# Second score and aggregation of later chunks behind the adjacency products; a leaving state added to x one half step later

## The chip, the cores and the metric

The kernel runs on one core of one Trainium2 chip. The metric is device time in microseconds, the median over runs of the whole program. TensorE does matrix products and transposes into PSUM, VectorE and ScalarE move and combine what stands there, POOL (GpSimd) does small work in SBUF, SyncE issues transfers.

## What is computed

Four layers on x of shape (128, 64, 256), each on a normalised, rectified copy of x and added to x: two attention layers with 8 heads, then a graph attention, then three steps of a gated recurrence. The change touches the last two. Cut from the reference:

```
h = maximum(layernorm(x), 0)                     # third layer
h = h @ W
s1, s2 = h @ a1, h @ a2
e = leaky_relu(s1[:, :, None] + s2[:, None, :], 0.2) * mask
x = x + elu(softmax(e) @ h + beta * h)
h = maximum(layernorm(x), 0)                     # fourth layer
for _ in range(3):
    av = concat([adj @ h, adj @ h])
    z = sigmoid(lin(av, w3) + lin(h, u3))
    r = sigmoid(lin(av, w4) + lin(h, u3))
    hv = tanh(lin(av, w5) + lin(r * h, u5))
    h = (1 - z) * h + z * hv
x = x + h
```

## The kernel before

The 8192 rows are 64 tiles of 128, taken as 16 chunks of 4 tiles. The first two layers run over all chunks (to about 610 us). The graph layer of chunks 0 and 1 is done on the way, and that of chunks 2 to 15 inside the recurrence. Every fp32 product is made as three products of high and low parts (`product`, L91), so one 256x256 weight on a chunk is 12 matmuls of 512 columns. ScalarE writes the high part, VectorE the low part (`..._hi`, `..._lo`).

The recurrence works on 8 groups of two chunks, in halves. A group has 6 halves (k = 1 to 5, then 0 of the next group; `Half`, L395), two for each of the three steps; even k belongs to the first chunk of the group, odd k to the second. While TensorE makes the sums of one chunk, the gates of the other are finished: each `half` ends half k-1's state with u5 and begins its own half with u3. The order on each engine is written out by hand in one function `half` per engine (ScalarE L898, VectorE L1360, TensorE L1759); `Half` says which chunk's graph work goes into which half. Engines wait for each other by counting semaphores alone.

On TensorE a half is: transposes of the state (halves 2 to 5, `ring` banks 0 and 1), u3 (12 matmuls, `ring` banks 2 and 3, named hu afterwards), adjacency (64 matmuls of 64x64 tiles into `scores`, L1706), u5 on r*h of the other chunk, w4 (sum of r, `ring` 0 and 1), w3 (sum of z, `scores` 0 and 1), w5 (`scores` 2 and 3). Between these stand the graph pieces of a later chunk: `graph_rows` (transposes, L1659), `graph_product` for four tiles (the product with W and both score columns, `g_hT` with `g_w`, alternately in `ring` 2 and 3), `graph_s2` (the second score spread over rows, 16 matmuls of 64x64 tiles, L1671), `graph_attT` (4 transposes of the attention, L1679), `graph_aggregate` (16 matmuls of 64x64 tiles, attT with hw, L1690). A chunk that enters the recurrence is transposed by `enter` (L1648), one that leaves by L1847.

On VectorE: `r*h` (L1369) and rh_lo, `graph_low`, `agg_low`, statistics for a normalisation (`rows_stats`, L1203), `update` of the state in two parts (L1322 to L1327, three operations each), `r_sum`, the low part of h (L1397), `z_sum`, `graph_scores` (L1226 to L1235: sum, leaky relu, mask, maximum), `graph_attention` (L1239 to L1246: total, reciprocal, att), `copy_attT` (L1253), `graph_positive` and `graph_negative` (y added to x), `leave` (state added to x). On ScalarE: copies of the transposed state (`tok`, printed as later_w), rhp_hi, tanh of z, copies hu, `graph_high`, `agg_high`, tanh of hv, `copy_hw` (L827), high part of h, `r_tanh` (L881), `graph_read` and `graph_exp` (y), `norm_rows`. POOL shifts the scores by their maximum (`g_shift`) and makes the scale of a normalisation.

## Time and profile before

| what | value |
|---|---|
| median of 3 runs | 1502.7 us (1502.57 to 1502.71) |
| the profiled execution's own time | 1503.36 us |
| its span | 1501.6 us |
| TensorE matmul busy, share of the span | 98% |
| TensorE weight load | 82% |
| VectorE | 83% |
| ScalarE | 66% |
| POOL | 36% |
| mean granted TensorE clock | 0.991 of full speed |

Busy times are sums over the span; a matmul's end is modelled and matmuls overlap, so pitches are read from the starts in the timeline. A wait of TensorE shows as idle time in front of a row, with what ended it behind an arrow. In the rows `ring` and `scores` are the two PSUM tensors; `later_w` is the memory that tok, z and the exponential of y share.

### The profile page before, as it was taken

To read this page: it belongs to the slowest core of one execution; us is meant where nothing else is said; L and a number is where in the kernel's file an instruction comes from. 1 tells how busy PE (TensorE), PEld (TensorE's weight loads), DVE (VectorE), ACT (ScalarE), POOL (GpSimd) and SP (SyncE) were. 2 spreads that over 40 slices of the span, in tenths; PEclk is the share of its full clock that TensorE was granted. 3 is DMA by queue.
4 is the path that set the end of the run, shared out by engine and by line. 5 is a ranking of instruction groups with operands and counts; after the bars stand their busy time and mean duration, and the time that the engine had idled before them with its cause. 6 is when DMAs were issued, how large, how long until landed. Compare 5 with 4: busy or idle time off the path is not lost.

```text
span 1501.6 us, 45862 instructions
## 1 busy us (share of the span) xinstructions
PE 1464.4 (98%) x18922; PEld 1237.2 (82%) x18922; DVE 1244.5 (83%) x2517; ACT 990.1 (66%) x1795; POOL 538.7 (36%) x623
## 2 busy tenths in 40 slices
PE   8999999899999997799999999999999999999997
PEld 7898999899888886688888788887887887887886
DVE  4888877989999998888888888888888888888767
ACT  5767767667777776666666666666666666666564
POOL 3876776767888885411101101111111111111000
PEclk9999999999999999899999999999999999999999
DMA  8300000002333234100000000000000000000000
GB/s 267 87 2 0 0 0 2 16 17 45 65 68 65 56 58 59 29 1 1 29 1 2 30 1 1 30 1 1 30 1 1 30 1 1 29 2 1 29 2 28
DMA packets 36839, 40.89 MB, mean 27 GB/s; under 512 B 11872, under 2 KB 31840, under 8 KB 36704
## 3 DMA queue, kind: packets, MB, share of 16 engines
q0 software_dynamic: 4608, 16.78, 5.9%
q1 hardware_dynamic: 32096, 22.10, 4.9%
q8 instruction: 111, 1.82, 0.5%
q14 instruction: 24, 0.20, 0.0%
HBM read 13.71 MB, written 8.39 MB: 15 GB/s over the span
## 4 chain that ended last, share of the span: by engine, by line
PE 91%; DVE 5%; ACT 1%; POOL 1%; issue 1%; DMA 0%; DVEq 0%; POOLq 0%
PE ring L99 43%; PE scores L99 28%; PE scores L1706 3%; PE ring L1506 3%; PE scores L1470 3%; PE ring L1546 2%; PE ring L1775 2%; PE ring L1517 2%; PE ring L1690 1%; PE ring L1847 1%; PE ring L1648 1%; PE ring L1659 1%; PE ring L1671 1%; DVE s L1035 1%; PE ring L1679 0%
## 5 line engine op out<-in xcount | busy, mean ns | idle before, releaser
L543 POOL TENSOR_TENSOR s<-s,mx 128x512 f32<-128x512 f32 x128 | 138.2, 1103 | 56.8 <-DVE mx L1040 56.8
L617 POOL TENSOR_TENSOR r_var_eps<-r_mean_var,eps 128x4 f32<-128x4 f32 x16 | 8.1, 508 | 377.1 <-DVE r_mean_var L1208 377.1
L549 POOL TENSOR_TENSOR s<-s,rtotal 128x512 f32<-128x512 f32 x128 | 130.8, 1059 | 31.6 <-DVE rtotal L1046 31.4
L701 ACT ACTIVATE s<-s 128x512 f32<-128x512 f32 x128 | 77.9, 642 | 69.0 <-POOL s L543 68.8
L1371 DVE TENSOR_TENSOR rhp_lo<-r,rhp_hi 128x1024 fp32r<-128x1024 f32 x47 | 57.6, 1225 | 73.4 <-ACT rhp_hi L916 73.4
L1035 DVE SCALAR_TENSOR_TENSOR s<-scores,mask 128x512 f32<-128x512 f32 x128 | 87.1, 681 | 30.6 <-PE scores L1470 30.6
L881 ACT ACTIVATE r<-r,bias_half 128x512 f32<-128x512 f32 x96 | 64.3, 717 | 58.9 <-DVE r L1342 58.9
L935 ACT ACTIVATE hv<-scores,bias 128x512 f32<-128x512 f32 x94 | 64.7, 689 | 55.0 <-PE scores L99 55.0
L909 ACT ACTIVATE later_w<-ring 128x512 f32<-128x512 f32 x64 | 34.8, 596 | 99.0 <-PE ring L1775 99.0
L713 ACT ACTIVATE pT<-ring 128x512 f32<-128x512 f32 x128 | 66.1, 603 | 42.4 <-PE ring L1506 42.4
L1040 DVE TENSOR_REDUCE mx<-s 128x8 f32<-128x512 f32 x128 | 87.9, 686 | 4.4
L1333 DVE TENSOR_TENSOR agg_lo<-scores,agg_hi 128x512 fp32r<-128x512 f32 x96 | 61.8, 685 | 32.7 <-ACT agg_hi L874 32.3
L1044 DVE TENSOR_REDUCE total<-s 128x8 f32<-128x512 f32 x128 | 82.5, 645 | 0.0
L99 PE MATMUL ring<-agg_hi,w4T_hi 128*128 128x512 f32 x192 | 78.2, 407 | 2.3 <-DVE agg_lo L1333 2.3
L99 PE MATMUL scores<-rhp_hi,u5T_hi 128*128 128x512 f32 (+1 forms) x192 | 80.3, 418 | 0.0
L99 PE MATMUL scores<-agg_hi,w5T_hi 128*128 128x512 f32 (+1 forms) x192 | 78.3, 408 | 0.0
L617 POOL TENSOR_TENSOR g_var_eps<-g_mean_var,eps 128x4 f32<-128x4 f32 x16 | 8.3, 519 | 192.7 <-DVE g_mean_var L1208 192.7
L99 PE MATMUL scores<-agg_hi,w3T_hi 128*128 128x512 f32 x192 | 77.2, 402 | 0.0
L99 PE MATMUL scores<-agg_hi,w3T_lo 128*128 128x512 f32 x192 | 75.8, 395 | 0.0
L99 PE MATMUL scores<-agg_lo,w3T_hi 128*128 128x512 f32 x192 | 75.8, 395 | 0.0
L99 PE MATMUL ring<-agg_hi,w4T_lo 128*128 128x512 f32 x192 | 75.8, 395 | 0.0
L99 PE MATMUL ring<-agg_lo,w4T_hi 128*128 128x512 f32 x192 | 75.7, 394 | 0.0
(314 smaller groups left out, 5129.8 us busy)
## 6 DMA issues: line engine op xcount, KB each, us to landing
x<-beta_less_one POOLq DMA_DIRECT2D x16, 512.0 KB, 4.7
x<-o POOLq DMA_DIRECT2D x16, 512.0 KB, 6.6
out_x<-x SPq DMA_DIRECT2D x15, 512.0 KB, 2.9
x<-in_x SPq DMA_DIRECT2D x1, 6144.0 KB, 25.4
later_w<-in_L_gnn_w_w SPq DMA_DIRECT2D x3, 512.0 KB, 6.4
x<-in_x SPq DMA_DIRECT2D x2, 512.0 KB, 5.3
x<-in_x SPq DMA_DIRECT2D x1, 1024.0 KB, 7.4
stage<-in_L_gnn_w_qkv SPq DMA_DIRECT2D x3, 256.0 KB, 3.1
```

The source lines that it names most:

```text
L99: last = pe.matmul(out, s, m, start=(begins and n == 0), stop=(ends and n == len(terms) - 1))
L543: pool.tensor_tensor(sr, sr, mx[:, r, :].unsqueeze(2).to_broadcast([P, CT * 2, N]), ALU.subtract).then_inc(s_shifted, 1)
L549: pool.tensor_tensor(sr, sr, rtotal[:, r, :].unsqueeze(2).to_broadcast([P, CT * 2, N]), ALU.mult).then_inc(p_ready, 1)
L701: act.activation(s[:, par, r, :, :, :], s[:, par, r, :, :, :], ACT.Exp).then_inc(p_exp, 1)
L713: act.activation(pT[:, r, :, :].rearrange("p t q -> p (t q)"), ring[:, r, :], ACT.Copy).then_inc(pT_copied, 1)
L881: act.activation(r[:, m, :], r[:, m, :], ACT.Tanh, bias=bias_half[:, 1, m:m + 1], scale=0.5)\
L935: act.activation(hv[:, m, :], high[:, 2 + m, :], ACT.Tanh, bias=bias[:, 2, m:m + 1])\
L1035: dve.scalar_tensor_tensor(sr(par, r), scores[:, r, :].rearrange("p (a k) -> p a k", k=N), SCALE, masks[layer_of(i, lay)][:].unsqueeze(1). ...
L1040: dve.reduce_max(mx[:, r, :], sr(par, r), AX.X).then_inc(s_max, 1)
L1044: dve.reduce_sum(total[:, r, :], sr(par, r), AX.X).then_inc(p_total, 1)
L1333: dve.tensor_tensor(agg.lo[:].rearrange("p m (t g q) -> p g m t q", t=CT, g=2)[:, g], high[:, g, :].rearrange("p (m t q) -> p m t q", m=FT ...
L1371: dve.tensor_tensor(rhp.lo[:], r[:], f32(rhp.hi[:]), ALU.subtract).then_inc(rh_lo_ready, 1)
```

## The change

In `Half`, the second score and the attention of a chunk (`graph_s`) stay in halves 2 and 4, the aggregation and all behind it (`graph_b`) move to halves 3 and 5. `graph_s2` and `graph_aggregate` stand right behind the adjacency products. The transposes of the attention stand behind w5 in `ring` bank 3, where u3 of the next half writes its second part. In halves with graph products w4 comes first, then two graph products, w3, two graph products, w5; ScalarE makes all four copies of hw behind tanh of r. ScalarE copies hu in front of each tanh of z. The final transposes of a leaving state stand behind w5 in banks 0 and 1, and VectorE adds them to x in the next half, between r*h and rh_lo. Statistics of a chunk for the recurrence come behind the low part of h (half 3) or the sum of z (half 5); the odd chunk's rows are normalised in half 0 and not in half 5.

The diff, cut to the table of halves and to the functions `half` of ScalarE, VectorE and TensorE. Left out are the first half of all (a semaphore of its own for its copies of hu), waits that moved from helpers to their callers, and `final_rows`, which holds the loop of the final transposes as before with the bank as an argument.

```diff
-self.left = group * 2 - 2 if self.k == 0 and not self.first else None
-self.left_before = group * 2 - 1 if self.k == 1 and not (fixed and group == 0) else None
+self.left = None
+if self.k == 0 and not self.first:
+    self.left = group * 2 - 2
+if self.k == 1 and not (fixed and group == 0):
+    self.left = group * 2 - 1
 self.later = group * (HALVES - 2) + self.k
 self.before_step = STEPS - 1 if self.k == 0 else (self.k - 1) // 2
...
 even, odd = group * 2 + 2, group * 2 + 3
 self.graph_a = {1: even, 3: odd}.get(self.k) if goes_on else None
-self.graph_b = {2: even, 4: odd}.get(self.k) if goes_on else None
+self.graph_s = {2: even, 4: odd}.get(self.k) if goes_on else None
+self.graph_b = {3: even, 5: odd}.get(self.k) if goes_on else None
+self.y_bank = 2 if self.k == 3 else 0
 self.graph_stats = {0: even, 1: odd}.get(self.k) if goes_on else None
 self.graph_norm = {0: even, 2: odd}.get(self.k) if goes_on else None
 self.stats = {3: even, 5: odd}.get(self.k) if goes_on else None
-self.norm = {4: even, 5: odd}.get(self.k) if goes_on else None
-self.after_a = {2: even, 4: odd}.get(self.k) if goes_on else None
-self.after_b = {3: even, 5: odd}.get(self.k) if goes_on else None
+self.norm = {4: even}.get(self.k) if goes_on else None
+if self.k == 0 and not self.first and not self.last:
+    self.norm = group * 2 + 1
...
     act.activation(rhp.hi[:], r[:], ACT.Copy).then_inc(rh_hi_ready, 1)
     for m in range(FT):
+        act.wait_ge(hu_ready, n * FT + m + 1)
+        act.activation(hu[:, m, :], ring[:, 2 + m, :], ACT.Copy).then_inc(hu_copied, 1)
         act.wait_ge(z_added, (n - 1) * FT + m + 1)
         act.activation(z[:, m, :], z[:, m, :], ACT.Tanh, bias=bias_half[:, 0, m:m + 1], scale=0.5)\
             .then_inc(z_done, 1)
-    if not s.last:
-        act.wait_ge(hu_ready, n * FT + 1)
-        act.activation(hu[:, 0, :], ring[:, 2, :], ACT.Copy).then_inc(hu_copied, 1)
-    if s.graph_b is not None:
-        g_exponential(s.graph_b)
-    if not s.last:
-        act.wait_ge(hu_ready, (n + 1) * FT)
-        act.activation(hu[:, 1, :], ring[:, 3, :], ACT.Copy).then_inc(hu_copied, 1)
     if s.graph_a is not None:
         graph_high(s.graph_a)
-    if not s.last:
-        agg_high(n)
+    agg_high(n)
+    if s.graph_b is not None:
+        graph_read(s.graph_b, ring, s.y_bank)
+    if s.norm is not None and s.k == 0:
+        norm_rows(rn, r_hn[1], s.norm, 1, (agg_ready, (n - 4) * FT))
     for m in range(FT):
         act.wait_ge(hv_ready, (n - 1) * FT + m + 1)
         act.activation(hv[:, m, :], high[:, 2 + m, :], ACT.Tanh, bias=bias[:, 2, m:m + 1])\
             .then_inc(hv_done, 1)
-    if s.graph_a is not None:
-        copy_hw(s.graph_a, 0)
-        copy_hw(s.graph_a, 1)
-    if s.enters is not None:
+    if s.graph_b is not None:
+        graph_exp(s.graph_b)
+    if s.graph_s is not None:
+        g_exponential(s.graph_s)
+    if s.enters is not None and s.k != 0:
         enter(s.enters, s.other)
     if s.norm is not None and s.k == 4:
...
             act.activation(hp[s.other].hi[:, m, :], h[s.other][:, m, :], ACT.Copy)\
                 .then_inc(h_hi_ready, 1)
-    if not s.last:
-        r_tanh(n)
+    if s.enters is not None and s.k == 0:
+        enter(s.enters, s.other)
+    r_tanh(n)
     if s.graph_a is not None:
-        copy_hw(s.graph_a, 2)
-        copy_hw(s.graph_a, 3)
-    if s.graph_b is not None:
-        graph_out(s.graph_b)
-    if s.norm is not None and s.k == 5:
-        norm_rows(rn, r_hn[1], s.norm, 1, (agg_ready, (n - 3) * FT))
+        for t in range(CT):
+            copy_hw(s.graph_a, t)
     if s.graph_norm is not None:
         graph_normalise(s.graph_norm, 0 if s.k == 0 else 1)
...
     dve.wait_ge(r_done, n * FT)
     dve.scalar_tensor_tensor(r[:], r[:], 1.0, s.h_before()[:], ALU.add, ALU.mult).then_inc(rh_done, 1)
+    if s.left is not None:
+        leave(s.left, ring, 0)
+    if s.graph_b is not None:
+        copy_attT(s.graph_b, ring, 3)
     dve.wait_ge(rh_hi_ready, n)
     dve.tensor_tensor(rhp.lo[:], r[:], f32(rhp.hi[:]), ALU.subtract).then_inc(rh_lo_ready, 1)
...
         final_sum(T + 3, 1, 1)
         dve.wait_ge(x_final, CHUNKS)
-    if s.graph_b is not None:
-        graph_attention(s.graph_b)
     if s.graph_a is not None:
         graph_low(s.graph_a)
-    if not s.last:
         agg_low(n)
-    if s.stats is not None:
-        recurrence_stats(s.stats)
     if s.graph_stats is not None:
         rows_stats(gn, s.graph_stats)
+    if s.graph_a is None:
+        agg_low(n)
+    if s.graph_s is not None:
+        graph_scores(s.graph_s)
+    if s.graph_b is not None:
+        graph_positive(s.graph_b, ring, s.y_bank)
     dve.wait_ge(z_done, n * FT)
     update(s, 0)
     if s.graph_b is not None:
-        copy_attT(s.graph_b)
+        graph_negative(s.graph_b)
     update(s, 1)
-    if s.enters is not None:
+    if s.enters is not None and s.k != 0:
         enter(s.enters, s.other)
-    if not s.last:
-        r_sum(n)
+    r_sum(n)
+    if s.enters is not None and s.k == 0:
+        enter(s.enters, s.other)
     if s.before_step < STEPS - 1:
         for m in range(FT):
...
     if s.closing:
         close_rh(s)
-    if not s.last:
-        z_sum(n)
-    if s.graph_a is not None:
-        graph_scores(s.graph_a)
-    if s.graph_b is not None:
-        graph_out(s.graph_b)
-    if s.leaves is not None:
-        leave(s.leaves)
+    if s.graph_s is not None:
+        graph_attention(s.graph_s)
+    if s.k == 3 and s.stats is not None:
+        recurrence_stats(s.stats)
+    z_sum(n)
+    if s.k == 5 and s.stats is not None:
+        recurrence_stats(s.stats)
+    if s.closing:
+        leave(s.leaves, ring, 2)
...
         else:
             pe.wait_ge(h_lo_ready, (s.later - 1) * FT)
-        if s.left is not None:
-            pe.wait_ge(left, (s.left + 1) * 2)
-        if s.left_before is not None:
-            pe.wait_ge(left, (s.left_before + 1) * 2)
-        if s.left is None:
-            pe.wait_ge(hu_copied, n * FT)
-        if s.after_a is not None:
-            pe.wait_ge(e_sum, s.after_a + 1)
-        if s.after_b is not None:
-            pe.wait_ge(x_plus_pos, (s.after_b + 1) * 2)
+        if isinstance(n, int) and n == 1:
+            pe.wait_ge(first_hu_copied, FT)
+        else:
+            pe.wait_ge(hu_copied, (n - 1) * FT)
+        if s.graph_s is not None:
+            pe.wait_ge(hw_copied, (s.graph_s + 1) * FT)
         for m in range(FT):
+            if m == 1 and s.graph_b is not None:
+                pe.wait_ge(attT_copied, s.graph_b + 1)
             product(pe, ring[:, 2 + m, :], columns(wT["u3"], m), moving(hp[s.me])).then_inc(hu_ready, 1)
 
...
             if s.step == 0:
                 pe.wait_ge(r_added, n * FT)
+            if s.left is not None:
+                pe.wait_ge(left, (s.left + 1) * 2)
             graph_rows(s.graph_a)
         wait_apart(pe, z_added, n * FT)
         adjacency(r_hn[s.me] if s.step == 0 else tok)
+    if s.graph_s is not None:
+        wait_apart(pe, hu_copied, n * FT)
+        graph_s2(s.graph_s)
+    if s.graph_b is not None:
+        if s.y_bank == 2:
+            wait_apart(pe, hu_copied, n * FT)
+        graph_aggregate(s.graph_b, ring, s.y_bank)
     pe.wait_ge(rh_lo_ready, n)
     for m in range(FT):
         product(pe, high[:, 2 + m, :], columns(wT["u5"], m), moving(rhp), begins=False)\
             .then_inc(hv_ready, 1)
-    if s.enters is not None or s.graph_a is not None or s.graph_b is not None:
-        pe.wait_ge(hu_copied, (n + 1) * FT)
-    if s.enters is not None:
+    if s.enters is not None or s.graph_a is not None:
+        pe.wait_ge(hu_copied, n * FT)
+    if s.enters is not None and s.k != 0:
+        enter(s.enters, s.other)
+    pe.wait_ge(agg_lo_ready, (n + 1) * FT)
+    if s.step == 0 and s.graph_a is None:
+        pe.wait_ge(r_added, n * FT)
+        if s.left is not None:
+            pe.wait_ge(left, (s.left + 1) * 2)
+    if s.graph_b is not None and s.y_bank == 0:
+        pe.wait_ge(x_plus_pos, (s.graph_b + 1) * 2)
+    for m in range(FT):
+        product(pe, ring[:, m, :], columns(wT["w4"], m), moving(agg)).then_inc(r_ready, 1)
+    if s.enters is not None and s.k == 0:
         enter(s.enters, s.other)
     if s.graph_a is not None:
         pe.wait_ge(g_hT_lo_ready, (s.graph_a + 1) * FT)
+        if s.graph_b is not None:
+            pe.wait_ge(x_plus_pos, (s.graph_b + 1) * 2)
         graph_product(s.graph_a, 0)
         graph_product(s.graph_a, 1)
-    if s.graph_b is not None:
-        graph_attT(s.graph_b)
-    if not s.last:
-        pe.wait_ge(agg_lo_ready, (n + 1) * FT)
-        if s.step == 0 and s.graph_a is None:
-            pe.wait_ge(r_added, n * FT)
-        for m in range(FT):
-            product(pe, ring[:, m, :], columns(wT["w4"], m), moving(agg)).then_inc(r_ready, 1)
+    for m in range(FT):
+        product(pe, high[:, m, :], columns(wT["w3"], m), moving(agg)).then_inc(z_ready, 1)
     if s.graph_a is not None:
         pe.wait_ge(hw_copied, s.graph_a * FT + 1)
         graph_product(s.graph_a, 2)
         graph_product(s.graph_a, 3)
-    if s.graph_b is not None:
-        graph_aggregate(s.graph_b)
-    if not s.last:
-        for m in range(FT):
-            product(pe, high[:, m, :], columns(wT["w3"], m), moving(agg)).then_inc(z_ready, 1)
-    if s.graph_a is not None:
-        graph_s2(s.graph_a)
+    if s.closing:
+        pe.wait_ge(h_done, n * FT)
+        pe.wait_ge(hu_copied, n * FT)
+        final_rows(s, 2)
+        close_w5(s)
+        return
+    pe.wait_ge(hv_done, n * FT)
+    for m in range(FT):
+        product(pe, high[:, 2 + m, :], columns(wT["w5"], m), moving(agg), ends=False)
+    if s.graph_s is not None:
+        pe.wait_ge(e_sum, s.graph_s + 1)
+        graph_attT(s.graph_s, ring, 3)
     if s.leaves is not None:
         pe.wait_ge(h_done, n * FT)
-        if s.enters is not None:
-            pe.wait_ge(h0_lo_ready, (s.enters + 1) * FT)
-        elif not s.last:
-            pe.wait_ge(hu_copied, (n + 1) * FT)
-        else:
-            pe.wait_ge(left, s.leaves * 2)
-        for q in range(2):
-            for t in (2 * q, 2 * q + 1):
-                for f in range(FT):
-                    at = (t % 2) * D + f * P
-                    last = pe.transpose(ring[:, 2 + q, at:at + P],
-                                        h[s.other][:, f, t * P:(t + 1) * P], ident[:])
-            last.then_inc(final_ready, 1)
-    if s.closing:
-        close_w5(s)
-    else:
-        pe.wait_ge(hv_done, n * FT)
-        for m in range(FT):
-            product(pe, high[:, 2 + m, :], columns(wT["w5"], m), moving(agg), ends=False)
+        pe.wait_ge(r_added, (n + 1) * FT)
+        final_rows(s, 0)
```

What moves, in the order of instructions. First TensorE, half 2, around the adjacency products (L1706 before, L1715 after) and up to u5. Before:

```order
L1706 MATMUL scores<-adjT,later_w 64x64 [waits z_added,tok_copied]
L1706 MATMUL scores<-adjT,later_w 64x64 x31
L99 MATMUL scores<-rhp_hi,u5T_hi 128x512 [waits rh_lo_ready]
L99 MATMUL scores<-rhp_lo,u5T_hi 128x512
L99 MATMUL scores<-rhp_hi,u5T_lo 128x512
```

After:

```order
L1715 MATMUL scores<-adjT,later_w 64x64 [waits z_added,tok_copied]
L1715 MATMUL scores<-adjT,later_w 64x64 x31
L1681 MATMUL ring<-ident,hw 64x64 [waits hu_copied]
L1681 MATMUL ring<-ident,hw 64x64 x7
L99 MATMUL scores<-rhp_hi,u5T_hi 128x512 [waits rh_lo_ready]
```

The second score (ring<-ident,hw) of the chunk now stands between adjacency and u5; before, it stood between w3 and w5 of half 1.

Second, ScalarE in half 1, from tanh of hv to the copies of hw. Before:

```order
L935 ACTIVATE hv<-scores,bias 128x512 [waits hv_ready] x2
L826 ISA
L827 ACTIVATE hw<-ring 128x258 [waits hw_ready]
L826 REGISTER_ALU
L827 ACTIVATE hw<-ring 128x258 [waits hw_ready]
L947 ACTIVATE hp_a_hi<-h_a 128x512 [waits h_done] x2
L881 ACTIVATE r<-r,bias_half 128x512 [waits r_added] x2
```

After:

```order
L938 ACTIVATE hv<-scores,bias 128x512 [waits hv_ready] x2
L951 ACTIVATE hp_a_hi<-h_a 128x512 [waits h_done] x2
L887 ACTIVATE r<-r,bias_half 128x512 [waits r_added] x2
L832 ISA
L833 ACTIVATE hw<-ring 128x258 [waits hw_ready]
L832 REGISTER_ALU
L833 ACTIVATE hw<-ring 128x258 [waits hw_ready]
```

The first two copies of hw moved behind the high part of h and tanh of r.

Third, VectorE from the low part of h in half 2 to rh_lo in half 3. Before:

```order
L1397 TENSOR_TENSOR hp_b_lo<-h_b,hp_b_hi 128x512 [waits h_hi_ready]
L1347 TENSOR_TENSOR later_w<-scores,hu 128x512 [waits z_ready] x2
L1261 SCALAR_TENSOR_TENSOR x<-ring,x 128x2x256 [waits y_read]
L1261 ISA [waits y_read]
L1261 SCALAR_TENSOR_TENSOR x<-ring,x 128x2x256
L1272 TENSOR_TENSOR x<-x,later_w 128x1024 [waits y_exp_ready,x_plus_pos]
L1369 SCALAR_TENSOR_TENSOR r<-r,h_a 128x1024 [waits r_done]
L1371 TENSOR_TENSOR rhp_lo<-r,rhp_hi 128x1024 [waits rh_hi_ready]
```

After:

```order
L1407 TENSOR_TENSOR hp_b_lo<-h_b,hp_b_hi 128x512 [waits h_hi_ready]
L1240 TENSOR_REDUCE g_total<-e 128x4 [waits e_exp]
L1242 RECIPROCAL g_rtotal<-g_total 128x4 [waits e_total]
L1247 TENSOR_TENSOR att<-e,g_rtotal 64x4x64 [waits attT_ready,e_rtotal]
L1247 TENSOR_TENSOR att<-e,g_rtotal 64x4x64
L1351 TENSOR_TENSOR later_w<-scores,hu 128x512 [waits z_ready] x2
L1373 SCALAR_TENSOR_TENSOR r<-r,h_a 128x1024 [waits r_done]
L1254 TENSOR_TENSOR attT<-ring,beta_ident 128x512 [waits attT_ready,y_ready]
L1379 TENSOR_TENSOR rhp_lo<-r,rhp_hi 128x1024 [waits rh_hi_ready]
```

The attention (g_total to att) now stands ahead of the sum of z, and the copy of attT between r*h and rh_lo; y is added to x in half 3.

## Rows read from the trace of the kernel before

**Rows 1.** The page, busy time by engine: TensorE.

```profile
PE 1464.4 (98%) x18922; PEld 1237.2 (82%) x18922; DVE 1244.5 (83%) x2517; ACT 990.1 (66%) x1795; POOL 538.7 (36%) x623
```

**Rows 2.** Chain that ended last, 1000 to 1040 us: start us, us, piece.

```profile
1009.56 5.65 PE ring L99 x36
1015.22 2.79 PE scores L99 x12
1018.00 0.61 PE ring L1671 x16
1018.62 2.99 PE scores L99 x12
1021.61 0.87 PE ring L1775 x8
...
1025.25 1.09 PE scores L1706 x64
1026.34 2.99 PE scores L99 x12
1029.33 0.44 PE ring L1679 x4
...
1032.57 1.02 PE ring L1690 x16
1033.60 5.79 PE scores L99 x24
```

**Rows 3.** Timeline, TensorE, half 1 of two groups: start us, us, instruction.

```profile
966.97 1.16 PE L1706 MATMUL scores<-adjT,r_hn_b 64*64 64x64 f32 x64
...
1078.87 1.16 PE L1706 MATMUL scores<-adjT,r_hn_b 64*64 64x64 f32 x64
```

**Rows 4.** Timeline, ScalarE, half 1.

```profile
1075.86 1.32 ACT L919 ACTIVATE later_w<-later_w,bias_half 128x512 f32<-128x512 f32 x2
...
1083.06 0.69 ACT L935 ACTIVATE hv<-scores,bias 128x512 f32<-128x512 f32 x1 [0.70 <-PE scores L99]
...
1088.46 1.34 ACT L881 ACTIVATE r<-r,bias_half 128x512 f32<-128x512 f32 x2
1089.71 0.64 ACT L827 ACTIVATE hw<-ring 128x258 f32<-128x258 f32 x2
```

**Rows 5.** Timeline, VectorE, half 1.

```profile
1079.22 1.29 DVE L1217 TENSOR_TENSOR g_hT_lo<-ring,g_hT_hi 128x512 fp32r<-128x512 f32 x2 [2.01 <-ACT g_hT_hi L823]
1080.70 1.29 DVE L1333 TENSOR_TENSOR agg_lo<-scores,agg_hi 128x512 fp32r<-128x512 f32 x2 [0.18 <-ACT agg_hi L874]
1081.90 1.40 DVE L1203 BATCH_NORM_STATS2 g_stats<-x 128x6 f32 x4
...
1083.64 0.66 DVE L1322 TENSOR_TENSOR hv<-hv,h_a 128x512 f32<-128x512 f32 x1
...
1087.74 1.28 DVE L1342 TENSOR_TENSOR r<-ring,hu 128x512 f32<-128x512 f32 x2
```

**Rows 6.** Timeline, VectorE and ScalarE, the graph layer's steps in halves 3 and 4.

```profile
1018.76 0.86 DVE L1226 TENSOR_TENSOR e<-ring,hw 64x256 f32<-64x256 f32 x2
...
1020.90 1.22 DVE L1369 SCALAR_TENSOR_TENSOR r<-r,h_b 128x1024 f32<-128x1024 f32 x1
...
1026.15 0.42 DVE L1239 TENSOR_REDUCE g_total<-e 128x4 f32<-128x256 f32 x1 [0.79 <-ACT e L833]
...
1026.82 0.85 DVE L1246 TENSOR_TENSOR att<-e,g_rtotal 64x256 f32<-64x256 f32 x2
...
1036.67 1.06 ACT L844 ACTIVATE later_w<-later_w 128x1024 f32<-128x1024 f32 x1
```

**Rows 7.** Timeline, four transposes without and with a stop ahead of them.

```profile
1029.17 0.60 PE L1679 MATMUL ring<-ident,att 128*128 128x128 f32 x4
...
1495.82 0.42 DVE L1314 SCALAR_TENSOR_TENSOR h_b<-hv,h_b 128x256 f32<-128x256 f32 x1
...
1496.30 0.66 PE L1756 MATMUL scores<-ident,h_b 128*128 128x128 f32 x4 [1.79 <-DVE h_b L1314]
```

More of the change, by code:

```diff
@@ L337, in network @@
         hu_ready = sem("hu_ready")
+        first_hu_copied = sem("first_hu_copied")
         hu_copied = sem("hu_copied")
@@ L1278, in enter, with leave @@
                                           ALU.subtract).then_inc(h0_lo_ready, 1)
-                def leave(c, psum=ring, bank=2):
+                def leave(c, psum, bank):
                     for q in range(2):
@@ L1338, in r_sum @@
                 def r_sum(n):
-                    dve.wait_ge(hu_copied, (n + 1) * FT)
+                    if isinstance(n, int) and n == 0:
+                        dve.wait_ge(first_hu_copied, FT)
+                    else:
+                        dve.wait_ge(hu_copied, n * FT)
                     for m in range(FT):
@@ L1729, in begin, with final_rows @@
                         product(pe, high[:, 2 + m, :], columns(wT["w5"], m), moving(agg), ends=False)
-                    pe.wait_ge(hu_copied, FT)
+                    pe.wait_ge(first_hu_copied, FT)
                     enter(1, 1)
+                def final_rows(s, bank):
+                    for q in range(2):
+                        for t in (2 * q, 2 * q + 1):
+                            for f in range(FT):
+                                at = (t % 2) * D + f * P
+                                last = pe.transpose(ring[:, bank + q, at:at + P],
+                                                    h[s.other][:, f, t * P:(t + 1) * P], ident[:])
+                        last.then_inc(final_ready, 1)
                 def close_w5(s):
@@ L1782, in half @@
                             pe.wait_ge(h_lo_ready, (s.later - 1) * FT)
-                        if s.left is not None:
-                            pe.wait_ge(left, (s.left + 1) * 2)
-                        if s.left_before is not None:
-                            pe.wait_ge(left, (s.left_before + 1) * 2)
-                        if s.left is None:
-                            pe.wait_ge(hu_copied, n * FT)
-                        if s.after_a is not None:
-                            pe.wait_ge(e_sum, s.after_a + 1)
-                        if s.after_b is not None:
-                            pe.wait_ge(x_plus_pos, (s.after_b + 1) * 2)
+                        if isinstance(n, int) and n == 1:
+                            pe.wait_ge(first_hu_copied, FT)
+                        else:
+                            pe.wait_ge(hu_copied, (n - 1) * FT)
+                        if s.graph_s is not None:
+                            pe.wait_ge(hw_copied, (s.graph_s + 1) * FT)
                         for m in range(FT):
+                            if m == 1 and s.graph_b is not None:
+                                pe.wait_ge(attT_copied, s.graph_b + 1)
                             product(pe, ring[:, 2 + m, :], columns(wT["u3"], m), moving(hp[s.me])).then_inc(hu_ready, 1)
@@ L1871, in _ @@
                     graph_product(0, t, high, 2)
+                pe.wait_ge(hw_copied, FT)
                 graph_s2(0, high, 2)
@@ L1880, in _ @@
                 graph_product(1, 1, high, 0)
+                pe.wait_ge(attT_copied, 1)
                 graph_aggregate(0, high, 2)
@@ L1884, in _ @@
                 graph_product(1, 3, high, 0)
+                pe.wait_ge(hw_copied, 2 * FT)
                 graph_s2(1, high, 0, hw_next)
```

5 lines of the change are left out of this document (2 added, 3 removed).

## The prediction

> **What bounds the kernel now.** I read the busy times first. TensorE is busy for 1464.4 of 1501.6 us, all other engines for less [rows 1]. A busy TensorE is not one at its peak, since matmuls overlap, so I read next the chain that ended last over two halves of a middle group. It is TensorE without a hole: 12 matmuls of one product take 2.79 us, another piece of TensorE work follows at once, and nothing waits for VectorE or ScalarE [rows 2]. A gain must therefore come from TensorE's own pitch. A loss comes from any result that VectorE or ScalarE delivers later than TensorE comes for it. So I read when ScalarE and VectorE do what the moved steps need, from the adjacency products on [rows 3 to 6], and what a stop costs TensorE [rows 7].
>
> I count halves 1 to 5 and 0 inside a group as the source does with k, and call A the start of the adjacency products in a half. Seven groups carry attention of later chunks, two chunks each: 14 chunks.
>
> **What it saves.** A product of full 128x128 matmuls takes 2.79 us, but 2.99 us right behind the second score (16 matmuls of 64x64 tiles, 0.61 us), and behind the adjacency products too; two products behind the aggregation take 5.79 us, 0.20 more than twice 2.79 [rows 2]. So each excursion to small tiles costs 0.20 us beside its own work, about 0.10 on the way in and 0.10 on the way out (my split). The adjacency products make this excursion anyway, so the second score and the aggregation behind them save 0.20 us each. The transposes of the attention take 0.44 us where 4 of 8 transposes (0.87 us, of which 0.09 is a like start-up) take 0.35 [rows 2]. Ahead of the state's transposes, which are of the same kind, they save that 0.09. Per chunk 0.20 + 0.20 + 0.09 = 0.49 us, for 14 chunks 6.9 us. Moving the final transposes behind w5 saves nothing in halves 5 and 0: they still stand ahead of one full product. TensorE's work is otherwise the same.
>
> The Trainium skill ("TensorEngine Tiling (Array Packing)", Key Properties) says that a change of tiling mode drains the engine, which agrees with the 0.20 us in kind. Its page "TensorE: Matmul & The Clock Gate" (Single matmul latency) gives an isolated warm matmul some 166 ns beyond its columns. If each way in and each way out cost that much, the two moved steps would save 0.66 us a chunk and not 0.40, 3.6 us more in all, by an estimate from that page; the trace has 0.20 for both ways, and the sum goes by it.
>
> **What it makes late, in halves 1 and 3.** TensorE's third and fourth graph products overwrite the banks of the first two, so they wait until ScalarE has copied those. Before, ScalarE copied them right behind tanh of hv. Now the copies stand behind tanh of r, and only the w3 product lies between the product pairs. From A, TensorE wants the third graph product at 1.09 (adjacency) + 2.90 (u5, with the way out) + 2.80 (w4) + 1.43 (first pair) + 2.80 (w3) = 11.02 us; the pair is (5.65 - 2.79) / 2 [rows 2].
> Half 1: with A at 1078.87 [rows 3] that is 1089.89. Tanh of r began at 1088.46, because it needs the sum of r, which VectorE reaches only at 1087.74 behind statistics and both state updates [rows 4, 5]. The copies behind it end at 1089.71 + 0.64 = 1090.35, and a result takes 0.06 us to TensorE (h_b ends at 1496.24, the transposes start at 1496.30) [rows 4, 7]. Late by 0.52 us. Also new: the second tanh of z, half of 1.32 us [rows 4], now stands ahead of ScalarE's high part of g_hT. That puts VectorE's g_hT_lo from 1079.22 to about 1079.9 and agg_lo, 1.2 behind it, from 1080.70 to 1081.1; all that follows on VectorE shifts by 0.4 [rows 5]. **Wait in half 1: 0.9 us.**
> Half 3: the aggregation (1.02 us [rows 2]) stands ahead of u5, so the third product is wanted at A + 12.04. VectorE: agg_lo at A + 2.23 as in half 1 after the change, then in steps of 1.20 (1080.70 to 1081.90 [rows 5]) the positive part of y at 3.43 and the first update at 4.63. A state update takes 2.05, half of 1083.64 to 1087.74 [rows 5], so the negative part could start at 6.68. Its exponential comes later. The second tanh of hv started 4.19 behind A (1083.06 [rows 4]), now 5.21, and the exponential of y (1.06 us [rows 6]) runs to about 6.9. Negative part 6.9 to 8.05, second update from there. Tanh of r starts 2.77 behind an update's start (1085.69 to 1088.46 [rows 4, 5]), at 10.8; copies end 1.25 + 0.64 later and reach TensorE at 12.8. **Wait in half 3: 0.74 us.**
>
> **Halves 2 and 4, into 3 and 5.** VectorE now makes the scores between agg_lo and the updates, the attention behind the sum of r and the low part of h, and copies attT behind the next r*h. From A: agg_lo 1.83 (1078.87 to 1080.70), + 1.20, scores and maximum + 2.14 (1018.76 to 1020.90), two updates + 4.10, sum of r + 1.20, low part of h + 1.20 = 11.67; attention 1.52 (1026.15 to 1026.82 + 0.85), done at 13.2 [rows 3, 5, 6]. TensorE, with the second score, wants it at 1.09 + 0.61 + 2.90 + 3 x 2.80 = 13.0: late by 0.25. Behind the attention VectorE still has the sum of z (1.20), r*h (1.15 of its 1.22) and attT (0.69): attT reaches TensorE at 16.33. TensorE wants to overwrite its bank with the second half of u3 at 13.0 + 0.35 + 0.79 + 1.49 = 15.63. This later wait contains the earlier one. **0.69 us for each of halves 2 and 4.** The shift of the scores on POOL and their exponential on ScalarE, two operations on 256 elements, lie in the 6 us that this leaves between maximum and attention, and I take them as hidden. The second score itself waits for the second copy of hu, which ScalarE makes right behind u3, while the adjacency products (1.09 us) run; I take it as in time.
>
> **Half 5 and half 0** get no wait, narrowly. The aggregation adds 1.02 to TensorE. VectorE runs positive part, updates with the negative part between (second one at 8.05), entry, r, z, statistics (1.74 [rows 5]), r*h, the leaving rows (1.2) and rh_lo, ready near A + 19.1, where TensorE wants it near 19.16. The leaving rows were added at the end of the half before and fill an idle time of VectorE now. Their store is a transfer behind the same semaphore and ends nothing. SP and POOL queues keep their order.
>
> **Sum.** Waits per group 0.9 + 0.74 + 2 x 0.69 = 3.0 us, saved 0.98: + 2.06, times 7 = 14.4 us. Each stop also loses the weights loaded ahead: four transposes took 0.66 us behind a stop, 0.60 without one [rows 7]. Six stops a group, 42 x 0.06 = 2.5 us. Bounds for this: nothing, up to 0.15 us each (6 us), since a full matmul behind a stop is not shown; I take the row that is there. Total + 16.9 us on the profiled execution's 1503.4 us, which stands 0.7 us above the median of 1502.7: **1519.6 us.** Each wait may be 0.15 us off (28 of them, 4 us); with the stops' bounds the case holds 1512 to 1527.
> The Trainium skill ("TensorE: Matmul & The Clock Gate", LDWEIGHTS) has a weight load of 128 columns at some 107 ns. Were each stop to pay it whole, an estimate from that page is 4.5 us for stops, and 1521.6 us; the one row speaks for less.
>
> **Rivals.**
> 1. *Only the switches count.* If the chains on VectorE and ScalarE are shorter than I read them, by 0.7 to 0.9 us each, no wait arises and 6.9 us are won: 1495.8 us. It decides where waits stay under 0.98 us a group. For it: TensorE waits nowhere in the groups today. Against it: VectorE's operations follow each other in these halves without a gap, so I see no slack to absorb it. 10%.
> 2. *Half of the waits.* The attention comes in time (updates or scores overlap better) and only halves 1 and 3 wait: 7 x (1.64 - 0.98) + 14 x 0.06 = + 5.5, 1508 us. 15%.
> 3. *The narrow places go over.* rh_lo in half 0, and agg_lo there, come 0.2 us late each (+ 2.8) and a stop costs 0.15 (+ 3.8 more): 1526 to 1531 us. 10%.
>
> **Chances.** The forecast's case has 65%. "The same" is within 0.2%, 3 us, about what a measurement of this kernel tells from no change. Faster 0.10 is rival 1; same 0.04 the lower edge of rival 2; slower 0.86. For 8 times in 10 the range takes the case and most of rival 2: 1507 to 1527 us.
>
> **What would show it.** In the profile after: TensorE's small-tile excursions in halves 2 to 5 gone; new TensorE waits for the copies of hw by ScalarE, two per group, of 0.7 to 1.0 us; for att 0.25 and for attT 0.4 us on VectorE, two of each; a group of 114.0 us instead of 111.9 (966.97 to 1078.87 [rows 3]). It is wrong if a group is shorter than 111.9 us, or if TensorE waits mostly for something else, such as hu or rh_lo.

## The result, and the profile after

The changed kernel takes 1525.8 us (median; 1524.6 to 1527.3), the kernel before 1502.7 us on the same chip: ratio 1.0153, 95% interval 1.014 to 1.0166. That is slower, within the range given, 6.2 us above the forecast of 1519.6. The profiled execution has a span of 1524.1 us against 1501.6.

TensorE's busy time on the page hardly changed [rows 1]; the span grew around it.

```profile
PE 1466.4 (96%) x18922; PEld 1234.6 (81%) x18922; DVE 1247.3 (82%) x2517; ACT 990.7 (65%) x1795; POOL 529.7 (35%) x623
```

The chain that ended last, over halves 2 and 3 of a middle group of the changed kernel (start us, us, piece). Before, it was TensorE alone [rows 2].

```profile
1002.71 1.00 DVE hv L1325
1003.73 0.69 DVE h_b L1328
...
1010.00 0.42 DVE att L1247
1010.45 0.81 DVE later_w L1351 x2
1011.26 0.40 issue
1011.66 1.21 DVE r L1373
1012.87 0.61 DVE attT L1254
1013.48 0.04 issue
1013.53 1.67 PE ring L99 x6
...
1026.74 1.31 ACT r L887 x2
1028.05 0.56 ACT hw L833 x2
1028.65 1.71 PE ring L99 x12
```

It now runs over VectorE through the updates, the attention and attT, and in half 3 over ScalarE's tanh of r and the copies of hw. TensorE's waits in the whole program (waiting line, releaser: us in total, times, longest) have two new entries; the first contains one wait of 1.6 us that was there before, outside the groups:

```profile
PE ring L1689 <- DVE att L1247: 11.9, 15, 1.6
PE ring L99 <- ACT hw L833: 9.4, 14, 1.0
```

And the timeline of TensorE in a group, from adjacency product to adjacency product of half 1 (start us, us, instruction; in brackets the idle time ahead and what ended it):

```profile
976.90 1.16 PE L1715 MATMUL scores<-adjT,r_hn_b 64*64 64x64 f32 x64
...
988.75 0.39 PE L99 MATMUL ring<-g_w_hi,g_hT_hi 128*128 128x258 f32 x1 [0.68 <-ACT hw L833]
...
990.30 0.39 PE L99 MATMUL scores<-agg_hi,w5T_hi 128*128 128x512 f32 x1
...
996.81 1.16 PE L1715 MATMUL scores<-adjT,later_w 64*64 64x64 f32 x64
997.80 0.65 PE L1681 MATMUL ring<-ident,hw 64*64 64x64 f32 x16
...
1010.57 0.63 PE L1689 MATMUL ring<-ident,att 128*128 128x128 f32 x4 [0.73 <-DVE att L1247]
1011.04 1.04 PE L1794 MATMUL ring<-ident,h_b 128*128 128x128 f32 x8
...
1015.04 1.03 PE L1670 MATMUL ring<-ident,g_hn 128*128 128x128 f32 x8
1016.00 1.16 PE L1715 MATMUL scores<-adjT,later_w 64*64 64x64 f32 x64
...
1028.65 0.39 PE L99 MATMUL ring<-g_w_hi,g_hT_hi 128*128 128x258 f32 x1 [0.61 <-ACT hw L833]
...
1091.99 1.16 PE L1715 MATMUL scores<-adjT,r_hn_b 64*64 64x64 f32 x64
```

This group takes 1091.99 - 976.90 = 115.09 us, 3.19 more than before [rows 3], and 7 x 3.19 = 22.3 us is about the whole difference of the spans (22.5). Four places hold it: both hw waits, the att wait, and u3 behind it, whose second half waits for attT (from 1011.83 to 1015.04, 3.21 us where 2.90 is normal).

### The profile page after: what moved, and what is told of

Same layout as the page of the kernel before. It is cut to its first block, busy times and chain, and to the rows that moved or that the text cites. A ratio compares the mean times of both kernels' runs of the same rounds, so it can differ in the third digit from the quotient of the medians.

```text
span 1524.1 us, 45896 instructions
## 1 busy us (share of the span) xinstructions
PE 1466.4 (96%) x18922; PEld 1234.6 (81%) x18922; DVE 1247.3 (82%) x2517; ACT 990.7 (65%) x1795; POOL 529.7 (35%) x623
## 4 chain that ended last, share of the span: by engine, by line
PE 53%; DVE 26%; issue 7%; ACT 7%; POOL 5%; DVEq 0%; DMA 0%; POOLq 0%; ACTq 0%
PE ring L99 26%; PE scores L99 15%; DVE hv L1325 3%; DVE hv L1323 2%; DVE total L1045 2%; PE scores L1715 2%; PE ring L1517 2%; PE scores L1481 2%; POOL s L549 2%; PE ring L1557 1%; POOL rstd L540 1%; DVE r L1346 1%; DVE agg_lo L1334 1%; DVE stats L1017 1%; DVE r L1373 1%
## 5 line engine op out<-in xcount | busy, mean ns | idle before, releaser
L634 POOL TENSOR_TENSOR e<-e,g_mx 128x256 f32<-128x256 f32 x16 | 16.0, 1001 | 190.7 <-DVE g_mx L1236 190.7
L99 PE MATMUL scores<-rhp_lo,u5T_hi 128*128 128x512 f32 (+1 forms) x192 | 75.5, 393 | 0.0
```

The lines of the kernel that those rows point to most:

```text
L99: last = pe.matmul(out, s, m, start=(begins and n == 0), stop=(ends and n == len(terms) - 1))
```

## The experiments

Each kernel is the changed kernel with an edit, unless it says otherwise. Ratios are to the kernel before, run beside it; its median was 1502.6 to 1504.1 us in these series, so times of different experiments are better compared by their ratios.

**1. The copies of hw early.** ScalarE copies hw tiles 0 and 1 between the two high parts of h, ahead of tanh of r:

```diff
                 .then_inc(h_hi_ready, 1)
+        if s.graph_a is not None and m == 0:
+            copy_hw(s.graph_a, 0)
+            copy_hw(s.graph_a, 1)
...
     if s.graph_a is not None:
-        for t in range(CT):
-            copy_hw(s.graph_a, t)
+        copy_hw(s.graph_a, 2)
+        copy_hw(s.graph_a, 3)
```

> The changed kernel, but ScalarE copies the first two hw tiles between the two high parts of h, ahead of tanh of r. Theory (TensorE's lost time is its waits, and this one is the late copy): both waits of a group for hw, 0.83 + 0.11 us in half 1 and 0.76 + 0.12 us in half 3 of the changed kernel's trace, go, and nothing else moves: 14 times 0.9 us less, 1513 us. Rival (the graph products would be held by something else at the same moment, such as the hand-over of the banks, or the wait only moves to half 2's attention): less than 4 us gained, 1522 us or more.

Measured: 1511.7 us, ratio 1.0057 [1.0041, 1.0074]. The hw waits are gone and the att wait stands:

```profile
PE ring L1692 <- DVE att L1250: 11.7, 15, 1.6
```

So these waits and their stops cost 13 to 14 us of the 23: the mechanism and its size hold.

**2. The attention early.** VectorE makes the attention between the two state updates, not behind the low part of h:

```diff
+    if s.graph_s is not None:
+        graph_attention(s.graph_s)
     update(s, 1)
...
-    if s.graph_s is not None:
-        graph_attention(s.graph_s)
```

> The changed kernel, but VectorE makes the attention between the two state updates instead of behind the low part of h. Theory as I put it in the prediction (the wait for attT contains the wait for att, because one unbroken chain on VectorE ends with the copy of attT): TensorE no longer waits 0.89 us for att, but 1.2 us for attT, and the time stays within 3 us of 1525.8. Rival (the two waits are separate costs): 14 times 0.9 us less, 1513 us.

Measured: 1525.4 us, 1.0146 [1.0129, 1.0163]. The wait only moved, from att to attT, which stands behind the same work of VectorE. Att is in time now, and u3 alone is 1.23 us late (4.13 us where 2.90 is normal), as much as att and attT together in the changed kernel:

```profile
PE ring L99 <- DVE attT L1254: 13.7, 14, 1.0
PE ring L99 <- ACT hw L833: 9.0, 14, 0.7
```

**3. attT early.** VectorE copies attT behind the sum of z of the same half, ahead of r*h:

```diff
+    z_sum(n)
+    if s.graph_s is not None:
+        copy_attT(s.graph_s, ring, 3)
...
-    if s.graph_b is not None:
-        copy_attT(s.graph_b, ring, 3)
```

> The changed kernel, but VectorE copies attT right behind the sum of z, ahead of r*h. Theory: only the part of the wait for attT that stands behind the wait for att goes, about 0.32 us in each of halves 3 and 5: 14 x 0.32 = 4.5 us less, 1521 us, with the wait for att unchanged at 0.9 us. Rival (the copy was the whole reason): 14 x 1.2 = 17 us less, 1509 us.

Measured: 1524.9 us, 1.014 [1.0123, 1.0157]; one us came back, not five. Half 3's hw wait took most of it: TensorE arrives earlier there, and what it waits for comes no earlier. The rest went to half 0, where rh_lo is now a tenth of a microsecond late.

```profile
PE ring L99 <- ACT hw L833: 12.0, 14, 1.0
PE ring L1689 <- DVE att L1247: 10.9, 15, 0.7
```

**4. All three.** 

> The changed kernel with all three edits: copies of hw early, attention between the updates, attT ahead of r*h. Theory: all TensorE waits of the groups go, and what is left is the saving alone. In the changed kernel's trace adjacency with the second score takes 1.56 us where it stood at 1.71 in sum, with the aggregation 1.96 where 2.12, so a chunk saves 0.15 + 0.15 beside my 0.49: 14 x 0.76 = 10.7 us under the kernel before, 1492 us, a group of 110.4 us. Rival (waits only move to the next late result, or the new order costs TensorE by itself): 1500 us or more.

Measured: 1506.1 us, 1.0022 [1.0012, 1.0032]: the expectation was wrong by 14 us. Once TensorE no longer stops in halves 1 to 4, it reaches half 0, half 3 and half 5 early, and finds results late there that had been in time (in half 5, 0.28 us in front of w4, which the list does not show):

```profile
PE scores L99 <- DVE rhp_lo L1380: 3.9, 7, 0.6
PE ring L99 <- issue: 2.7, 4, 1.0
PE ring L1702 <- ACT hu L925: 1.7, 7, 0.3
```

**5. Tanh of z behind.** ScalarE makes both tanh of z behind the high parts of g_hT and agg, and behind the read of y:

```diff
     for m in range(FT):
         act.wait_ge(hu_ready, n * FT + m + 1)
         act.activation(hu[:, m, :], ring[:, 2 + m, :], ACT.Copy).then_inc(hu_copied, 1)
-        act.wait_ge(z_added, (n - 1) * FT + m + 1)
-        act.activation(z[:, m, :], z[:, m, :], ACT.Tanh, bias=bias_half[:, 0, m:m + 1], scale=0.5)\
-            .then_inc(z_done, 1)
     if s.graph_a is not None:
         graph_high(s.graph_a)
     agg_high(n)
     if s.graph_b is not None:
         graph_read(s.graph_b, ring, s.y_bank)
+    for m in range(FT):
+        act.wait_ge(z_added, (n - 1) * FT + m + 1)
+        act.activation(z[:, m, :], z[:, m, :], ACT.Tanh, bias=bias_half[:, 0, m:m + 1], scale=0.5)\
+            .then_inc(z_done, 1)
```

> The changed kernel, but ScalarE makes both tanh of z behind its high parts (and behind reading y), not between and behind the copies of hu. It tests a term of my sum, 0.4 us in half 1 and the same in half 3, for the second tanh of z ahead of the high part of g_hT. Theory: agg_lo starts 1.83 us behind the adjacency products and not 2.17, so both waits for hw shrink by 0.34 us: 14 x 0.34 = 4.8 us less, 1521 us. Rival (the late tanh of z delays the tanh of hv and the state update as much): within 2 us of 1525.8.

Measured: 1528.9 us, 1.0169 [1.0151, 1.0187], worse than the change alone. Half 1's wait for hw fell by 0.33 us, where the prediction has 0.4, from 0.68 to

```profile
989.37 0.39 PE L99 MATMUL ring<-g_w_hi,g_hT_hi 128*128 128x258 f32 x1 [0.35 <-ACT hw L833]
```

but half 3's rose from 0.61 to 1.03, and rh_lo in half 0 came 0.3 late. In half 3 this is not the next narrow place but the rival of the expectation: both tanh of z now stand behind the read of y, tanh of hv behind them, and VectorE stands still ahead of the first update until tanh of hv is there. The update began 4.56 us behind the adjacency products in the changed kernel (1020.56) and begins 5.17 behind them here, and the third product follows 0.42 us later (timeline):

```profile
1021.79 0.69 DVE L1324 TENSOR_TENSOR hv<-hv,h_a 128x512 f32<-128x512 f32 x1 [0.85 <-ACT hv L939]
```

**6. Without POOL's shift.** POOL works on one score in 64:

```diff
-    pool.tensor_tensor(e[:], e[:], g_mx[:].unsqueeze(2).to_broadcast([P, CT, N]),
+    pool.tensor_tensor(e[:, :, 0:1], e[:, :, 0:1], g_mx[:].unsqueeze(2),
                        ALU.subtract).then_inc(e_shifted, 1)
```

> The changed kernel, but POOL subtracts the maximum from one score of 64 in each row and leaves the others as they are, so the softmax of the graph layer lacks its shift (this part is left out); the order of all engines stays. It tests why att came at A + 13.6 and not at A + 13.2: the middle operation of the first state update took 0.99 us beside POOL's shift (1002.15 to 1003.14) where it takes 0.69 otherwise. Theory (VectorE is slowed while POOL works on the same memory): that operation takes 0.7 us again, att is 0.3 us earlier, 14 x 0.3 = 4 us less, 1521.6 us. Rival (the operation was late for another reason, such as its wait for z): it stays at 0.99 and the time within 2 us of 1525.8.

Measured: 1520.6 us, 1.0116 [1.0097, 1.0134], as expected. In the changed kernel VectorE's second operation of the update takes 0.99 us while POOL shifts, timelines of both:

```profile
1002.71 0.99 DVE L1325 SCALAR_TENSOR_TENSOR hv<-later_w,hv 128x512 f32<-128x512 f32 x1
1003.73 0.69 DVE L1328 SCALAR_TENSOR_TENSOR h_b<-hv,h_b 128x512 f32<-128x512 f32 x1
...
1002.15 0.99 POOL L634 TENSOR_TENSOR e<-e,g_mx 128x256 f32<-128x256 f32 x1 [17.37 <-DVE g_mx L1236]
```

Without the shift it takes 0.69 (timeline), and the att wait, less the one outside the groups, falls from (11.9 - 1.6) / 14 = 0.74 to (6.8 - 0.7) / 14 = 0.44 us (TensorE's waits):

```profile
1000.27 0.69 DVE L1325 SCALAR_TENSOR_TENSOR hv<-later_w,hv 128x512 f32<-128x512 f32 x1
```

```profile
PE ring L1689 <- DVE att L1247: 6.8, 15, 0.7
```

**7. Experiment 4 with tanh of z behind.** 

> The kernel with the three edits, plus tanh of z behind the high parts. In the three-edit kernel a group takes 112.36 us and TensorE waits 0.45 us in half 3 for the copy of hu ahead of the aggregation, because r*h and all behind it on ScalarE come later. Theory: this wait goes, nothing else: 7 x 0.45 = 3 us less than 1506.1, 1503 us. Rival (the copy of hu is late by the r*h and not by the tanh of z between): no gain, 1506 us.

Measured: 1500.3 us, 0.9978 [0.9969, 0.9988]: 0.2% faster than before. The waits for hu and in half 5 are gone and one is left (TensorE's waits); a group takes 111.24 us (timeline).

```profile
PE scores L99 <- DVE rhp_lo L1381: 3.7, 7, 0.5
```

```profile
964.48 1.16 PE L1719 MATMUL scores<-adjT,r_hn_b 64*64 64x64 f32 x64
...
1075.72 1.16 PE L1719 MATMUL scores<-adjT,r_hn_b 64*64 64x64 f32 x64
```

**8. In addition the leaving rows behind rh_lo.**

```diff
-    if s.left is not None:
-        leave(s.left, ring, 0)
     dve.wait_ge(rh_hi_ready, n)
     dve.tensor_tensor(rhp.lo[:], r[:], f32(rhp.hi[:]), ALU.subtract).then_inc(rh_lo_ready, 1)
+    if s.left is not None:
+        leave(s.left, ring, 0)
```

Beside it, agg_lo stands ahead of the graph layer's statistics in every half.

> As the run with three edits and tanh of z behind, plus, on VectorE in half 0: the leaving rows added behind rh_lo and not ahead of it, and the statistics behind agg_lo. The three-edit kernel waits 0.62 us there for rh_lo, 0.08 us for agg_lo: one of the narrow places of the prediction, which the waits of the changed kernel had covered. Theory: TensorE then waits only in half 5 (0.28 us ahead of w4), and a group takes near 111.9 - 1.5 + 0.4 = 110.8 us: 7 x 1.1 = 8 us under the kernel before, 1495 us. Rival (a next late result comes up, for instance the state update behind the statistics): 1499 us or more.

Measured: 1507.9 us, 1.003 [1.0021, 1.004]. My theory fell: the rh_lo wait did not change, so the leaving rows do not cause it, and `graph_rows` in half 1, which overwrites their banks, now waits for them.

```profile
PE ring L1672 <- DVE x L1289: 4.1, 5, 1.5
PE scores L99 <- DVE rhp_lo L1379: 3.7, 7, 0.5
```

**9. The leaving state alone**, on the kernel before: `final_rows(s, 0)` behind w5, `leave(s.left, ring, 0)` between r*h and rh_lo of the next half, nothing of the graph layer moved.

> The kernel before with one part of the change alone: the final transposes of a leaving chunk stand behind w5 in banks 0 and 1, and VectorE adds them to x in the next half, between r*h and rh_lo. Everything of the graph layer stays where it was. Theory (as in the prediction): the moved rows fill an idle time of VectorE and TensorE has the same small work ahead of one full product, so nothing changes: 1503 us, within 1.5, and no new wait of TensorE. Rival: it brings the wait for rh_lo (0.5 us in half 0, and likewise half 1) that the combined kernels showed: 14 x 0.5 = 7 us, 1510.

Measured: 1505.8 us, 1.0014 [1.0005, 1.0023]: 2.1 us by the ratio, above the 1.5 us I allowed, though the interval begins at 0.8. No wait for rh_lo came. The one entry that grew is time in front of u3 of half 1, at the turn of the loop, in which TensorE waited for nothing that the profile shows:

```profile
PE ring L99 <- issue: 5.7, 4, 1.5
```

The kernel before and the changed one have 2.5 us there. The 3.2 us more are the whole difference of the spans (1504.7 against 1501.6), and a group without this gap takes 111.2 us in both: in the halves the move is free, as predicted.

**10. Experiment 7 with the odd chunk's statistics late:**

```diff
     dve.tensor_tensor(rhp.lo[:], r[:], f32(rhp.hi[:]), ALU.subtract).then_inc(rh_lo_ready, 1)
+    if s.k == 0 and s.norm is not None:
+        recurrence_stats(s.norm)
...
-    if s.k == 5 and s.stats is not None:
-        recurrence_stats(s.stats)
```

> The kernel with all three moves and tanh of z behind (1500.3 us), and the odd chunk's statistics for the recurrence (1.74 us on VectorE) moved from the end of half 5, ahead of r*h of half 0, to behind rh_lo in half 0. Theory: the one wait that is left in a group, 0.5 to 0.6 us for rh_lo in half 0, comes from r*h standing behind these statistics; it goes, 7 x 0.6 = 4 us: 1496 us, group 110.6 instead of 111.24. Rival: what needs the statistics (the rows that ScalarE normalises in half 0, and tanh of hv behind them) gets late and TensorE waits there instead: 1500 or more.

Measured: 1502.5 us, 0.9988 [0.9979, 0.9997], no faster than experiment 7. The statistics were the cause: the wait for rh_lo is gone. But the next product, w4, stopped instead in five of the groups, since agg_lo now stands behind two sets of statistics:

```profile
1063.08 0.49 PE L99 MATMUL ring<-agg_hi,w4T_hi 128*128 128x512 f32 x1 [0.55 <-DVE agg_lo L1338]
```

**11. And agg_lo ahead of the graph layer's statistics in half 0.**

```diff
-    if s.graph_stats is not None:
-        rows_stats(gn, s.graph_stats)
-    if s.graph_a is None:
-        agg_low(n)
+    agg_low(n)
+    if s.graph_stats is not None:
+        rows_stats(gn, s.graph_stats)
```

> The kernel before this one (three moves, tanh of z behind, the odd chunk's statistics behind rh_lo of half 0) with one change: in half 0 VectorE makes agg_lo ahead of the statistics of the next graph chunk, not behind them. In the last kernel TensorE's wait for rh_lo (0.54 us) was gone from half 0, but it waited 0.55 us for agg_lo, which ended 1.7 us later than ScalarE's high part allowed, behind these statistics; VectorE then idled 1.86 us. Theory: both waits are gone, nothing follows in their place, since the statistics fall into that idle time: a group is 0.65 us shorter than 111.87, 111.2 with the same gap at the loop's turn (1.0 us) and 110.6 with a gap of 0.4; total 1497 to 1498 us against 1502.5. Rival: the next graph chunk's rows, normalised on ScalarE from these statistics, get late and TensorE waits at their transposes in half 1: no gain, 1501 or more.

Measured: 1500.1 us, 0.9984 [0.9974, 0.9993]. TensorE's list of waits names no engine inside the middle groups any more, and a group without the gap at the loop's turn takes 110.0 us, against 110.8 in experiments 7 and 10 and 111.2 before. What is left is a tenth of a microsecond twice a group in the second half of u3 (2.99 us, where experiment 3 has 2.90), most likely for the copy of attT. Yet the time is that of experiment 7, not 1497. In the traced execution the gap at the loop's turn grew to

```profile
PE ring L99 <- issue: 6.2, 4, 1.9
```

from 1.8 us in experiment 7. Behind the longest of the four gaps, in which TensorE had stood still for 1.90 us, its granted clock fell to half (the 1.2 GHz level) for 3.4 us, and u3 took 4.35 us (timeline, and one microsecond of the table by windows, which ends with granted clock, DMA share, GB/s):

```profile
963.64 0.49 PE L99 MATMUL ring<-hp_b_hi,u3T_hi 128*128 128x512 f32 x1 [1.90 <-issue]
```

```profile
965.00:966.00 1.00, 1.00 (x4) 0.81 (x3) 0.68 (x1) 0.34 (x1) 0.00 (x0) 0.50 0.34 117
```

In no other trace here was the clock that low between 640 and 1490 us. These are single executions and not typical ones: the traced one of experiment 11 is the slowest of its 11 (1502.7 us, the others 1498.3 to 1501.9), that of experiment 7 the third fastest of its 10 (1499.0; 1497.8 to 1502.5). How much of the gap the medians hold is therefore not shown.

The records of transfers say more about the gap than its name, "issue". In each of the 52 gaps of the 13 traces, one 16 KB packet of the instruction queue is moved ahead of it, and TensorE goes on 1.7 to 2.0 us after that packet has landed. Ahead of the gap above it is the only transfer from 960.4 to 962.0 us (it starts at 960.5):

```profile
q8 instruction: 1, 0.02, 5.6%
```

The packet starts ahead of the gap by much the same time in all four turns of a kernel, by 2.5 us in the kernel before, 1.8 to 2.3 in most others, 1.7 in experiment 9 and 1.2 in experiment 11, and the later it starts the longer is the gap. So it looks as if TensorE waits there for the load of its next instructions. No run tests this, and what sets the start of the packet stays open.

## Why the prediction came out as it did

**Direction and mechanism: right.** The waits stand where the prediction put them, for hw in halves 1 and 3, for att at the end of halves 2 and 4, and for attT right behind. Per group, measured from TensorE's starts against the pitches without a stop; att and attT are 2 x (0.89 + 0.03 + 0.31), the late start, the stop and the late half of u3. The saving is 2 x 0.66, from the pitches given below the table, and the last row is what is left of 3.19:

| term, us per group | predicted | measured |
|---|---|---|
| saved on small tiles | -0.98 | -1.32 |
| hw, half 1, with its stop | 0.96 | 0.95 |
| hw, half 3, with its stop | 0.80 | 0.88 |
| att and attT, halves 2 and 4, with stops | 1.62 | 2.46 |
| the rest (w4 of half 0 some 0.1 late behind agg_lo, gap at the loop's turn 0.12) | 0 | 0.22 |
| sum | 2.40 | 3.19 |

**What it saves: under-sized.** The prediction took 0.20 us each for the second score and for the aggregation. They also pack more densely behind the adjacency products: adjacency and second score take 1.56 us (996.81 to 998.37) where the rows gave 1.09 + 0.61 = 1.70, and adjacency and aggregation 1.96 where they gave 1.09 + 1.02 = 2.11. That is 0.29 us more per chunk, of which 0.03 is lost again on what stands around them. The 0.09 us of the attention's transposes did not come: with nothing to wait for they take 0.44 us ahead of the state's transposes, and 0.35 + 0.09 before, the 0.09 in front of the first matmul of w4. The start-up is paid once for each group of transposes, also when another one follows (timeline of experiment 11):

```profile
1112.38 0.60 PE L1691 MATMUL ring<-ident,att 128*128 128x128 f32 x4
1112.82 1.04 PE L1796 MATMUL ring<-ident,h_b 128*128 128x128 f32 x8
```

With what it cost in front of it and behind it, the second score took 0.79 us before and adds 4.47 - 3.99 = 0.48 to adjacency and u5 now; the aggregation took 1.22 and adds 0.87. So a chunk saves 0.31 + 0.35 + 0.00 = 0.66 us and not 0.49, 2.4 us more in all than the forecast had, yet the time came out above it.

**Halves 1 and 3: right.** The third product came 0.83 and 0.76 us late, where 0.9 and 0.74 stood. Experiment 1 priced both at 14 us together; 7 x 1.83 is 12.8.

**Halves 2 and 4: the step that failed.** "The shift of the scores on POOL ... I take them as hidden." It ends in time itself, but it slows VectorE by 0.30 us on the very chain that makes the attention. Experiment 6 shows it: each of the 14 waits for att is 0.30 us shorter, 4.2 us in all, and the time 5 us. The kernel before shows the same collision from the other side, and I did not read it. There the shift ran beside VectorE's r*h, which began at 1020.90 and took 1.22 us [rows 6], and itself took half as long again (timeline of the kernel before, POOL):

```profile
1021.07 1.52 POOL L628 TENSOR_TENSOR e<-e,g_mx 128x256 f32<-128x256 f32 x1 [7.87 <-DVE g_mx L1235]
```

The Trainium skill ("SBUF — State Buffer", Who interferes with whom) has the rule: a VectorE instruction with two SBUF inputs contends with a GpSimd instruction that reads SBUF, and the order in which the two are issued decides which is blocked. Both traces agree: the one that began first kept its time (r*h 1.22 us before, the shift 0.99 us after), the other lost 0.30 to 0.53.
The rest of the error on att is small change: TensorE came 0.15 us earlier because of the denser packing, two updates took 4.21 us there without the shift (999.56 to 1003.77 in experiment 6) where half 1's row gave 4.10, and att needed 0.15 us to reach TensorE, not 0.06.

**"This later wait contains the earlier one": right.** In the changed kernel att was late by 0.89, its stop took 0.03, and attT held the second half of u3 for another 0.31, 1.23 us together; in experiment 2, with att in time, attT alone costs 1.23. (The terms of the prediction for attT add up to 16.30 and not 16.33, a difference of 0.4 us in all; and the group of 114.0 us that it announces leaves out its own stops, with them it is 114.3.)

**Stops: 0.06 us taken for each, 0.12 and 0.03 measured.** Two graph products behind a stop took 1.55 us (988.75 to 990.30) and not 1.43, four transposes 0.47 (1010.57 to 1011.04) where 0.44 is their pitch without a stop. The row chosen [rows 7] compared two summed durations, not two pitches. The weight load of the Trainium skill ("TensorE: Matmul & The Clock Gate", LDWEIGHTS), some 107 ns, is near what the stop in front of a graph product costs, and far above that of the transposes.

**Half 5 and half 0: right in this kernel, by luck of its stops.** The narrow places held because TensorE arrives late. In half 0 TensorE did stop for agg_lo, but for a tenth of a microsecond and not 0.2. Experiments 4, 7 and 10 show what the narrow places would have cost: 0.5 to 0.6 us a group. Rival 3 was wrong here, and is one reason why repairing the waits returned 20 us and no more at first. Rival 1, that only the switches count, gave 1495.8 us. The nearest to it is experiment 11, at 1500.1: its groups are 1.2 us shorter than before without the gap at the loop's turn, 8 us in seven, and in its traced execution the gap took 3.7 us of that back and the clock behind it 1.5.

## What to carry to other kernels

A move that shortens the bounding engine shifts its arrival everywhere behind, so cost it as a list of slacks in the order of the program: taking one wait away returns only the difference to the next narrow place, here 1 us of 5 in experiment 3. An operation put off to help one result is late for another, as tanh of z in experiment 5. Before calling a small operation hidden, ask what it runs beside on shared ports, and read in the trace whether the same instruction has two durations. Waits can be repaired by order alone, as experiments 7 and 11 do, if the queue of each engine is sorted by when TensorE wants the result.

## What the runs showed of the hardware

- VectorE's update operation with two SBUF inputs took 0.99 us and not 0.69 beside a GpSimd operation on SBUF; GpSimd's shift 1.52 and not 0.99 where VectorE had begun first.
- Two blocks of small tiles back to back run about 0.15 us shorter than the sum of their pitches apart (1.56 where 1.70 was, 1.96 where 2.11 was), beyond the 0.20 us of a way out and in. Four transposes ahead of eight others of the same kind save nothing (0.44 us).
- At the turn of the loop TensorE stood still for 0.3 to 1.9 us with nothing to wait for that the list of waits names. Each of these gaps ended 1.7 to 2.0 us after a 16 KB packet of the instruction queue had landed. Whether it is the cause is not tested.
- Behind a standstill of 1.90 us TensorE's granted clock was 0.50 for 3.4 us (experiment 11), and the 12 matmuls of u3 took 4.35 us and not 2.89.
